# Pixel attention of a hybrid block: projections by halves of the batches, scores over 32 rows

## What is computed

```python
def _prelu(x, a):
    return jnp.where(x >= 0, x, a * x)

def _conv1x1(x, w, b, a):
    y = jnp.einsum('oc,nchw->nohw', w, x) + b[None, :, None, None]
    return _prelu(y, a)

e1 = _conv1x1(x, w1, b1, a1).reshape(N, -1, HW)
e2 = _conv1x1(x, w2, b2, a2).reshape(N, -1, HW)
asm = _conv1x1(x, wa, ba, aa).reshape(N, C, HW)
score = jnp.einsum('nci,ncj->nij', e1, e2)
score = jax.nn.softmax(score, axis=2)
out = jnp.einsum('nij,ncj->nci', score, asm)
```

## Time and profile before

| | us |
|---|---|
| median of 3 runs | 677.83 |
| lowest and highest of them | 676.67, 680.13 |
| the profiled execution's own time | 678.65 |
| its span, first to last instruction | 676.8 |
| outside the span | 1.85 |

### The profile page before, as it was taken

How to read it: one execution, slowest core, us unless ns; L and a number is a source line. 1 busy time by engine, 2 the same in 40 slices (tenths; PEclk the granted TensorE clock), 3 DMA queues, 4 the chain that set the end, 5 groups by cost and what they waited for, 6 DMA issues and landing times.

```text
span 676.8 us, 10819 instructions
## 1 busy us (share of the span) xinstructions
PE 486.4 (72%) x3952; PEld 263.5 (39%) x3953; DVE 295.4 (44%) x713; ACT 332.7 (49%) x1109; POOL 8.6 (1%) x11
## 2 busy tenths in 40 slices
PE   5654555555797769999975566666657799899865
PEld 2221222223563456767732333333333344344411
DVE  1165000003884578888856000000002889548733
ACT  2332333333575367777752333333335767488533
POOL 0000000000000000000000000000002100000010
PEclk9555555555799889999996555555557999999977
DMA  4000000000000000000000000000001311000001
GB/s 197 0 2 0 1 1 0 1 1 0 0 1 2 0 0 2 2 1 1 1 1 0 1 0 1 1 0 1 0 1 29 69 40 32 1 1 2 1 5 37
DMA packets 8381, 7.44 MB, mean 11 GB/s; under 512 B 3202, under 2 KB 8066, under 8 KB 8196
## 3 DMA queue, kind: packets, MB, share of 16 engines
q1 hardware_dynamic: 8324, 6.70, 3.3%
HBM read 4.99 MB, written 0.52 MB: 8 GB/s over the span
## 4 chain that ended last, share of the span: by engine, by line
PE 57%; DVE 17%; ACT 16%; issue 7%; DMA 1%; DVEq 1%; SPq 1%; ACTq 0%
PE ps L328 17%; ACT arena L346 11%; PE ps L306 4%; PE ps L311 3%; PE ps L675 2%; PE ps L662 2%; PE ps L658 2%; PE ps L844 2%; PE ps L881 2%; PE ps L689 2%; DVE arena L1426 2%; PE ps L268 2%; DVE arena L1435 2%; PE ps L848 1%; PE ps L861 1%
## 5 line engine op out<-in xcount | busy, mean ns | idle before, releaser
L328 PE MATMUL ps<-arena,wsb 16*16 16x16 f32 (+1 forms) x1024 | 131.0, 206 | 117.0 <-ACT arena L346 111.4
L346 ACT ACTIVATE arena<-ps 16x16 f32<-16x16 f32 (+1 forms) x512 | 96.0, 188 | 192.0 <-PE ps L328 192.0
L328 PEld LDWEIGHTS ps<-arena,wsb 16*16 16x16 f32 (+1 forms) x1024 | 76.2, 118 | 200.3 <-ACT arena L346 186.9
L352 DVE TENSOR_TENSOR X<-X,ps 128x128 f32<-128x128 f32 x16 | 4.6, 287 | 199.3 <-PE ps L311 199.2
L1107 ACT ACTIVATE arena<-ps,arena 128x128 f32<-128x128 f32 (+1 forms) x128 | 52.3, 417 | 30.4 <-DVE arena L1427 30.3
L1225 ACT ACTIVATE arena<-ps 128x512 f32<-128x512 f32 x72 | 41.5, 599 | 15.5 <-PE ps L848 13.3
L1426 DVE TENSOR_REDUCE arena<-ps 128x2 f32<-128x512 f32 (+1 forms) x48 | 33.0, 688 | 17.7 <-PE ps L658 10.4
L675 PE MATMUL ps<-wsb,arena 128*128 128x128 f32 x192 | 30.7, 284 | 11.2 <-DVE arena L1435 11.2
L662 PE MATMUL ps<-arena 128*128 128x256 f32 x128 | 35.7, 402 | 0.0
L1435 DVE TENSOR_TENSOR arena<-arena 128x512 f32<-128x512 f32 x48 | 33.2, 692 | 1.6
L675 PEld LDWEIGHTS ps<-wsb,arena 128*128 128x128 f32 x192 | 22.3, 144 | 19.8 <-DVE arena L1435 18.0
(11 more groups left out here) (279 smaller groups left out, 770.7 us busy)
## 6 DMA issues: line engine op xcount, KB each, us to landing
wsb<-weights SPq DMA_DIRECT2D x1, 2060.5 KB, 9.3
arena<-w SPq DMA_DIRECT2D x20, 64.0 KB
arena<-xn SPq DMA_DIRECT2D x9, 128.0 KB, 2.6
wsb<-weights SPq DMA_DIRECT2D x1, 549.5 KB, 4.3
X<-x SPq DMA_DIRECT2D x1, 512.0 KB, 3.4
out<-arena SPq DMA_DIRECT2D x2, 256.0 KB, 2.3
arena<-w_biases SPq DMA_DIRECT2D x20, 17.0 KB
csb<-consts SPq DMA_DIRECT2D x1, 128.0 KB, 9.2
```

What stands on the lines that cost most here:

```text
L328: nc.tensor.matmul(step_columns(k, rows, r), w_state, states[0:rows, :, :, t].rearrange("p g j -> p (g j)"), start=False, stop=True, skip_ ...
L346: nc.scalar.activation(states[0:rows, :, :, t + 1].rearrange("p g j -> p (g j)"), step_columns(t // STEP_BANK, rows, t % STEP_BANK), func) ...
```

## The change

The six projections are issued in the order keys, queries, values of the first half of the batches, then values, keys, queries of the second, and each half needs only its own half of `xn`: `gn done` is signalled twice. ACT drains the key and query projections by halves, the value projection whole. DVE rectifies by halves of 512 columns. Ahead of the loop stand only the keys and queries of the first half; the two halves of the values follow in steps 0 and 1 behind the negated maxima, the second half's keys in step 2 and its queries in step 4. The masked copies and their tile `e2z` are gone: the scores contract over the 32 rows of the batch's own partition group, `queries[group]` and `keys[group]`. Values are turned in PE's step 3 and copied in ACT's step 4. The weights of the next attention are computed in DVE's steps 8 to 11.

The diff (in it the context of unchanged lines is as short as it was made):

```diff
@@ -575,26 +575,27 @@
                 mm = nc.tensor.matmul(ps[:, 0, i * P:(i + 1) * P], W("L2_A_" + w, HD), W(f"L2_B_{w}T", HD), start=True, stop=True)
             mm.then_inc(s["lora products"], 1)
 
-            pe.wait_ge(s["gn done"], 1)
-            for i, w in enumerate(("L1_w2T", "L1_w1T", "L1_waT")):
-                for h in range(2):
-                    nc.tensor.matmul(ps[:, 2 * i + h, :], W(w), halves(xn)[h], start=True, stop=True).then_inc(s["L1 proj"], 1)
-            queries = pm[:, 1, :].rearrange("p (j t) -> p j t", j=J)
+            for bank, w, h in ((6, "L1_w2T", 0), (7, "L1_w1T", 0), (4, "L1_waT", 0), (5, "L1_waT", 1), (3, "L1_w2T", 1), (2, "L1_w1T", 1)):
+                pe.wait_ge(s["gn done"], h + 1)
+                nc.tensor.matmul(ps[:, bank, :], W(w), halves(xn)[h], start=True, stop=True).then_inc(s["L1 proj"], 1)
+            keys, queries = (pm[:, i, :].rearrange("p (j t) -> p j t", j=J) for i in range(2))
             pe.wait_ge(s["L1 prelu"], 2)
             for b in range(B + 4):
                 if b < B:
 
-                    j, g = b // G, b % G
-                    if b < G:
-                        pe.wait_ge(s["L1 keys"], b + 1)
+                    j, group = b // G, slice(C * (b % G), C * (b % G) + C)
+                    if b == 2:
+                        pe.wait_ge(s["L1 biased"], 5)
+                    if b == B // 2:
+                        pe.wait_ge(s["L1 prelu"], 6)
                     if b >= 3:
                         pe.wait_ge(s["L1 exp"], b - 2)
                     for qt in range(TT):
-                        mm = nc.tensor.matmul(ps[:, b % 3, qt * T:(qt + 1) * T], queries[:, j, qt * P:(qt + 1) * P], e2z[:, g, j, :],
+                        mm = nc.tensor.matmul(ps[:, b % 3, qt * T:(qt + 1) * T], queries[group, j, qt * P:(qt + 1) * P], keys[group, j, :],
                                               start=True, stop=True)
                     mm.then_inc(s["L1 scores"], 1)
-                if b == 1:
-                    pe.wait_ge(s["L1 prelu"], 3)
+                if b == 3:
+                    pe.wait_ge(s["L1 prelu"], 4)
                     for jt in range(J * TT):
                         mm = nc.tensor.matmul(ps[:, 6 + jt // 4, (jt % 4) * P:(jt % 4 + 1) * P], pm[:, 2, jt * P:(jt + 1) * P],
                                               W("ident"), is_transpose=True, start=True, stop=True)
@@ -1056,10 +1057,11 @@
             nc.scalar.activation(rstd[:], mv[:, :, 1], ACT.Ln, bias=W("eps")).then_inc(s["gn log"], 1)
             act.wait_ge(s["gn log"], 1)
             nc.scalar.activation(rstd[:], rstd[:], ACT.Exp, scale=-0.5).then_inc(s["gn sigma"], 1)
-            for i, bias in enumerate(("L1_b2", "L1_b1", "L1_ba")):
-                act.wait_ge(s["L1 proj"], 2 * i + 2)
-                nc.scalar.activation(pr[:, i, :], ps[:, 2 * i:2 * i + 2, :].rearrange("p a b -> p (a b)"), ACT.Identity,
-                                     bias=W(bias)).then_inc(s["L1 biased"], 1)
+            for count, dst, bank, bias in ((1, halves(pr[:, 0, :])[0], ps[:, 6, :], "L1_b2"), (2, halves(pr[:, 1, :])[0], ps[:, 7, :], "L1_b1"),
+                                           (4, pr[:, 2, :], banks(4, 6), "L1_ba"),
+                                           (5, halves(pr[:, 0, :])[1], ps[:, 3, :], "L1_b2"), (6, halves(pr[:, 1, :])[1], ps[:, 2, :], "L1_b1")):
+                act.wait_ge(s["L1 proj"], count)
+                nc.scalar.activation(dst, bank, ACT.Identity, bias=W(bias)).then_inc(s["L1 biased"], 1)
             for b in range(B + 2):
                 if b < B:
                     act.wait_ge(s["L1 minus max"], b + 1)
@@ -1070,7 +1072,7 @@
                         ins = nc.scalar.activation(by_query1[:, b % 3, qt * T:(qt + 1) * T], ps[:, b % 3, qt * T:(qt + 1) * T], ACT.Exp,
                                                    bias=softmax1[:, b % 3, 1, qt:qt + 1], accum_out=softmax1[:, b % 3, 2, qt:qt + 1])
                     ins.then_inc(s["L1 exp"], 1)
-                if b == 1:
+                if b == 4:
                     act.wait_ge(s["values turned"], 1)
                     nc.scalar.activation(vt[:].rearrange("p a b -> p (a b)"), banks(6, 8), ACT.Copy).then_inc(s["values by token"], 1)
                 if b >= 2:
@@ -1345,32 +1347,29 @@
             for j in range(J):
                 ins = nc.vector.tensor_scalar(xn[:, j * T:(j + 1) * T], Xj[:, j, :], mv[:, j, 0:1], rstd[:, j:j + 1],
                                               ALU.subtract, ALU.mult)
-            ins.then_inc(s["gn done"], 1)
-
-            for i, w in enumerate("qkv"):
-                link(nc.vector.scalar_tensor_tensor(wqkv[:, i, :], lora[:, i, :], 2.0,
-                                                    W("block"), ALU.mult, ALU.mult))
-                link(nc.vector.tensor_tensor(wqkv[:, i, :], wqkv[:, i, :], W(f"L2_w{w}T"), ALU.add))
-            for i in range(2):
-                even = wqkv[:, i, :].rearrange("p (d two) -> p two d", two=2)
-                turned = wrot[:, i, :].rearrange("p (d two) -> p two d", two=2)
-                nc.vector.tensor_scalar(turned[:, 0, :], even[:, 1, :], -1.0, None, ALU.mult)
-                ins = nc.vector.tensor_copy(turned[:, 1, :], even[:, 0, :])
-            ins.then_inc(s["L2 weights"], 1)
-
-            def prelu(i, slope):
-                dve.wait_ge(s["L1 biased"], i + 1)
-                link(nc.vector.tensor_scalar(pm[:, i, :], pr[:, i, :], 0.0, W(slope), ALU.min, ALU.mult))
-                nc.vector.scalar_tensor_tensor(pm[:, i, :], pr[:, i, :], 0.0, pm[:, i, :], ALU.max, ALU.add)\
-                    .then_inc(s["L1 prelu"], 1)
-
-            prelu(0, "L1_a2")
-            prelu(1, "L1_a1")
-            dve.wait_ge(s["L1 prelu"], 1)
-            for g in range(G):
-                nc.vector.tensor_scalar(e2z[:, g, :, :].rearrange("p j t -> p (j t)"), pm[:, 0, :],
-                                        W("group_mask")[:, g:g + 1], None, ALU.mult).then_inc(s["L1 keys"], 1)
-            prelu(2, "L1_aa")
+                if j % 2 == 1:
+                    ins.then_inc(s["gn done"], 1)
+
+            def l2_weight(i):
+                link(nc.vector.scalar_tensor_tensor(wqkv[:, i, :], lora[:, i, :], 2.0, W("block"), ALU.mult, ALU.mult))
+                link(nc.vector.tensor_tensor(wqkv[:, i, :], wqkv[:, i, :], W("L2_w" + "qkv"[i] + "T"), ALU.add))
+
+            def turned_weights():
+                for i in range(2):
+                    even = wqkv[:, i, :].rearrange("p (d two) -> p two d", two=2)
+                    turned = wrot[:, i, :].rearrange("p (d two) -> p two d", two=2)
+                    nc.vector.tensor_scalar(turned[:, 0, :], even[:, 1, :], -1.0, None, ALU.mult)
+                    ins = nc.vector.tensor_copy(turned[:, 1, :], even[:, 0, :])
+                ins.then_inc(s["L2 weights"], 1)
+
+            def prelu(i, h, biased, slope):
+                dve.wait_ge(s["L1 biased"], biased)
+                out, y = halves(pm[:, i, :])[h], halves(pr[:, i, :])[h]
+                link(nc.vector.tensor_scalar(out, y, 0.0, W(slope), ALU.min, ALU.mult))
+                nc.vector.scalar_tensor_tensor(out, y, 0.0, out, ALU.max, ALU.add).then_inc(s["L1 prelu"], 1)
+
+            prelu(0, 0, 1, "L1_a2")
+            prelu(1, 0, 2, "L1_a1")
             for b in range(B + 1):
                 if b < B:
                     dve.wait_ge(s["L1 scores"], b + 1)
@@ -1380,6 +1379,16 @@
                     link(nc.vector.reduce_max(softmax1[:, b % 3, 0, :], ps[:, b % 3, :].rearrange("p (q k) -> p q k", q=TT), AX))
                     nc.vector.tensor_scalar(softmax1[:, b % 3, 1, :], softmax1[:, b % 3, 0, :], -1.0, None, ALU.mult)\
                         .then_inc(s["L1 minus max"], 1)
+                if b in (0, 1):
+                    prelu(2, b, 3, "L1_aa")
+                if b == 2:
+                    prelu(0, 1, 4, "L1_a2")
+                if b == 4:
+                    prelu(1, 1, 5, "L1_a1")
+                if 8 <= b < 11:
+                    l2_weight(b - 8)
+                if b == 11:
+                    turned_weights()
                 if b >= 1:
                     v = b - 1
                     dve.wait_ge(s["L1 exp"], v + 1)
```

## The result

The changed kernel takes **694.42 us** (median of four, 693.3 to 695.35) against 678.98 for the kernel before in the same comparison: a ratio of **1.0233, 95% interval 1.0186 to 1.0281**. The prediction was 677.1 with a range up to 690.5. The time lies above the range, and it is a loss of 2.3% where no measurable change was forecast.

What follows compares the result with a forecast made beforehand. In the loop DVE was taken to set the pace with PE close behind. The terms -5.7 + 1.95 + 1.1 + 1.9 gave -0.75 us, so 677.1 against the median 677.83; range 674.0 to 690.5.

Steps and rivals of the forecast that it cites:

- The clock in between: PE ahead of and in the loop: clock stays 1.00 from 168.6 us; a fall for a spell costs about +1.2 us.
- the cold loop: PE's clock stays at 0.50 through the loop: 690.5 us, or 684 for half of it; chance 0.33.
- the rival: The slower one: clock at 1.2 GHz through the loop, 3.1 us a batch, +13 us, 690.5; chance 0.33.
- I take 0.88: PE's 32-row scores in the loop: 0.88 us a batch, the same as the present 128-row ones.
- Front: Ahead of the loop: earlier projections, halves and no masked copies bring the first maxima from 178.30 to 172.6, -5.7 us.
- Halves between the first and fourth maxima: Three half rectifiers on DVE inside the loop's first steps: 7.4 us instead of 5.45, +1.95 us.
- The fourth half: The half rectifier in DVE's step 4 has nothing to hide in: +1.1 us.
- The weights: The next attention's weights in DVE's full steps: three pairs of 0.65 us, +1.9 us; four short ones in step 11, nothing.
- The cold spell of two batches: Clock falls in PE's wait for the first division, then rises: about +1.2 us over two batches, 678.3; chance 0.13.
- The faster rival: 32-row scores overlap neighbours, three 1.22 us DVE waits vanish: 673.4; chance 0.16 together with half rectifiers nearer their lower bound.
- The transposes' rule: Skill's sentence that transposes don't count as busy for the clock; hardly anything in the loop but value products would count.
- the slower rival: Clock stays at 1.2 GHz through the loop, PE 3.1 us a batch: +13 us, 690.5, or 684 for half; chance 0.33.

Runs made afterwards that it cites:

- The first two experiments: Scores over 128 rows, masking left out, in the changed kernel: 678.2 us, 1.0029; scores over 32 rows in the kernel before, masked copies still computed: 697.27 us, 1.0315.
- the first experiment: The changed kernel with scores contracting over all 128 rows and the masking left out (four batches' scores summed): 678.2 us, ratio 1.0029.
- the run with the weights ahead: The changed kernel with scores over 128 rows, masking left out, and the next attention's weights computed ahead of the loop: 674.77 us, ratio 0.9983.

## Why the prediction was wrong

**The step that failed** is "The clock in between": *the sum keeps 1.00 from 168.6 on*, and with it the chance of 0.33 for the cold loop. Measured, the clock was 0.50 from 173.8 us to near the end of the loop, so that PE set the pace with 3.5 us a batch where the sum had DVE's 1.95. The prediction saw the rival, its place and its sign, and had the row that spoke for it: 32-row and then 128-row work with PE busy 5.83 of 6.0 us and the clock down. It was outweighed by "the change leaves PE as many busy columns". That argument counted columns. The first two experiments show that at the same columns and as many loads the rows decide: 128 rows, 1.00, with PE busy 25.5 of 32 us; 32 rows, 0.50, with PE busy 48.0 of 48.

**The rival's price** was too small as well, 3.1 us a batch against 3.5. (Its sum, 13 x (3.1 - 1.95) - 0.75 - 1.2 = 13.0, gives 690.8 on 677.83; the prediction wrote 690.5.) Of the 0.4, most is the score. I took the 128-row score of the cold spell before, 1.71 us from its start to the transposes. PE of the kernel before in order of time:

```profile
180.20 1.91 PE L593 MATMUL ps<-arena 128*128 128x256 f32 x4
181.91 0.79 PE L609 MATMUL ps<-wsb,arena 128*128 128x128 f32 x4
```

That is a single instance. A 32-row one at the same clock takes 2.00. The transposes took 1.05 where I had 0.9. With the measured price the rival's own working gives 13 x (3.5 - 1.95) = 20.2, less 0.75 and 1.2, +18.2; the stage grew by 17.95. The range ended at 690.5 for want of these 0.4 us a batch: 13 x 0.4 = 5.2, which is 695.7.

**"I take 0.88"** for the 32-row score was at the wrong end as well: 1.06 at full clock. There it would hardly have mattered, by an estimate: 4 x (1.06 + 0.66) + 1.01 = 7.9 us of PE for four batches, against the pace of 7.8. At 1.2 GHz it counts in every batch.

**The sum's other terms held**, read in the first experiment, where nothing but the scores' rows differs from the kernel after. Front: -5.7 predicted, -5.4 there and -5.2 in the kernel after. Halves between the first and fourth maxima: +1.95 predicted, +1.9 (5.4 - 3.5). The fourth half: +1.1, 1.1 (3.5 - 2.4). A half rectifier: 1.10, 1.12. The weights: +1.9 predicted, measured +1.9 from the lead of 2.4 to 0.5, and 1.85 by taking them out. The cold spell of two batches, priced at 1.2 in "The clock in between", came in the run with the weights ahead and cost 1.12. Sum: -0.75 predicted; the stage was 0.54 shorter. The whole kernel's ratio there, 1.0029 (1.0001 to 1.0057), is some 0.4% above what the stage says (0.54 of 677.7 us less); where that comes from is open. The start of the stage alone differs by 2.0 us between the two profiles (163.47 and 161.50).

**One reading was wrong** and did no harm: the prediction counts three waits of 1.22 us for PE in the loop before. The trace has two, in steps 8 and 12; the third wait is the 0.99 in step 2. The faster rival was thus worth 2 x 1.22 = 2.4 us and not 3.7.

**Overlap of row groups** agrees with the trace: the Trainium skill (TensorE: Matmul & The Clock Gate, "Part 3: Packing small matmuls") says that matmuls in distinct row groups run at the same time. The twelve score records of batches 0 to 2 took 1.97 us against 2.75 over 128 rows in the first experiment, at clock 1.00 both. The same page's table ("Why this matters for your kernels") says that a lone 32-row matmul takes the time of a 128-row one. For the single record the traces agree, 374 ns against 379 at their shortest. From the score's start to the transposes behind it, its four records took 1.06 against 0.88, and 2.00 against 1.71. For the price of a batch that measurement decides.

**The transposes' rule** (same page, "Part 4: PE-mode transpose") leaned to the slower rival, and the prediction put it aside by a row. The slower rival came, but no run speaks for this reason: in the first experiment the loop has the same transposes and stays at 1.00 for 32 us. What differs is not the transposes but the rows of the scores between them.

**Open.** What about the rows of the scores the clock follows; why 64 rows, pairs of scores and the added 128-row matmuls bring 1.00 for a part of the loop or in some executions; and why PE's idle ahead of the first transposes drops the clock in one kernel and not in another. The last does not follow the rows: behind 32-row scores the clock fell about 2 us into an idle of 3.97 (kernel after), and behind 128-row scores an idle of 3.10 was followed by a fall in one run (the weights ahead of the loop) and by none in the first experiment.

## What to carry to other kernels

A contraction over fewer rows did not shorten TensorE's work here (1.06 us a score against 0.88) and took away what held its clock: price such a change with the loop at 1.2 GHz first, and take the loop at 2.4 GHz only if a row of the trace shows the clock held by work of that height. When the bound engine is relieved while its neighbour is at 90% busy, ask first what the neighbour costs at half its clock. What worked here was to keep the zeros and move their making to GpSimd, which had nothing to do in this stage (675.23 us, 0.9969 of before).

## What the runs showed of the hardware

- A stretch with PE busy 48.00 of 48.00 us at a granted clock of 0.50. Being busy alone did not bring 2.4 GHz: the same loop with 128-row scores was at 1.00 with PE busy 25.5 of 32 us.
- 32-row scores of two batches in different row groups take 2.08 us at clock 0.50, one batch's take 2.07; between 128-row transposes one batch's score costs 0.18 us more than a 128-row one at 1.00 (1.06 against 0.88), 0.29 at 0.50 (2.00 against 1.71, the latter from one instance).
- A GpSimd copy of 32 rows by 512 columns in fp32 took 0.76 us (3.04 for four), and of DVE's half rectifiers beside it the one-input instruction took 0.57 and 0.85 us instead of 0.48, and the two-input one 0.98 instead of 0.69.
